# Attention operands laid out by DMA through DRAM instead of by selector matmuls, with the column visits in neighbouring slots

## What is computed

```python
def _L0_attn_b_ref(x, Wq, bq, Wk, bk, Wv, bv, Wo, bo):
    q = (x @ Wq + bq).reshape(Bx, Tx, HEADS, HD)     # HEADS 16, HD 8
    k = (x @ Wk + bk)[:, :, None, :]
    v = (x @ Wv + bv)[:, :, None, :]
    q = _apply_rope(q, sin, cos, HD)
    k = _apply_rope(k, sin, cos, HD)
    att = jnp.einsum('bthd,bThd->bhtT', q, k) / math.sqrt(HD)
    att = jnp.where(causal, -jnp.inf, att)
    att = jax.nn.softmax(att, axis=-1)
    out = jnp.einsum('bhtT,bThd->bthd', att, v).reshape(Bx, Tx, Cx)
    return out @ Wo + bo

def expert_step(acc, w):                             # 8 experts, 128 -> 512 -> 128
    wg, wu, wd = w
    h = jax.nn.silu(x @ wg) * (x @ wu)
    return (acc + h @ wd, None)

x = x + _L0_attn_a_ref(_layernorm(x, axis=-1), ...)
x = x + _L0_ffn_ref(_layernorm(x, axis=-1), ...)
x = x + _L0_attn_b_ref(_layernorm(x, axis=-1), ...)
x = x + _L0_ffn_ref(_layernorm(x, axis=-1), ...)
```

## Time and profile before

| | us |
|---|---|
| median of three runs | 1626.02 |
| time of the profiled execution | 1626.96 |
| its span from the first to the last instruction | 1625.1 |
| PE busy with matmuls | 1492.9 (92%) |
| DVE busy | 1174.6 (72%) |
| ACT busy | 885.4 (54%) |
| POOL busy | 793.0 (49%) |
| one steady pass of the second half (five alike) | 101.2 |

### The profile page before, as it was taken

How to read it: one execution, slowest core, us unless ns; L and a number is a source line. 1 busy time by engine, 2 the same in 40 slices (tenths; PEclk the granted TensorE clock), 3 DMA queues, 4 the chain that set the end, 5 groups by cost and what they waited for, 6 DMA issues and landing times. The chain is left out here.

```text
span 1625.1 us, 23329 instructions
## 1 busy us (share of the span) xinstructions
PE 1492.9 (92%) x7504; PEld 1108.8 (68%) x7504; DVE 1174.6 (72%) x1943; ACT 885.4 (54%) x1520; POOL 793.0 (49%) x738
## 2 busy tenths in 40 slices
PE   2578899899989999899999999999999999999998
PEld 2355677677776777677567676776767767677786
DVE  4768786968778787868677585675857758577565
ACT  2244646464555556444655557565575655755554
POOL 2636544642535344531315546555465554655565
PEclk9689999999999999999999999999999999999999
DMA  6305534333344343433332334333343333433452
GB/s 182 136 1 175 201 133 153 134 139 150 123 148 147 134 155 117 156 117 117 117 131 103 118 117 146 124 133 117 118 154 123 126 117 121 157 119 124 148 182 112
DMA packets 36236, 216.28 MB, mean 133 GB/s; under 512 B 3475, under 2 KB 17300, under 8 KB 19732
## 3 DMA queue, kind: packets, MB, share of 16 engines
q1 hardware_dynamic: 36116, 214.79, 36.4%
HBM read 200.10 MB, written 15.27 MB: 133 GB/s over the span
## 5 line engine op out<-in xcount | busy, mean ns | idle before, releaser
L530 POOL TENSOR_TENSOR HL<-HF,HH 128x512 fp32r<-128x512 f32 x312 | 416.8, 1336 | 474.3 <-ACT HH L706 473.2
L1213 DVE TENSOR_TENSOR HF<-SG,bank 128x512 f32<-128x512 f32 x512 | 350.0, 684 | 170.3 <-PE bank L874 90.4
L872 PE MATMUL bank<-XTH,W 128*128 128x512 f32 x1024 | 422.8, 413 | 10.4 <-ACT SG L699 9.9
L874 PE MATMUL bank<-XTH,W 128*128 128x512 f32 x1024 | 403.1, 394 | 0.0
L873 PE MATMUL bank<-XTL,W 128*128 128x512 f32 x1024 | 402.7, 393 | 0.0
L1196 DVE SCALAR_TENSOR_TENSOR SG<-SG,bank 128x512 f32<-128x512 f32 x288 | 197.1, 684 | 207.4 <-ACT SG L701 205.6
L701 ACT ACTIVATE SG<-bank 128x512 f32<-128x512 f32 x288 | 172.1, 597 | 317.8 <-PE bank L874 316.3
L706 ACT ACTIVATE HH<-HF 128x512 fp32r<-128x512 f32 x512 | 320.4, 626 | 36.4 <-DVE HF L1213 32.0
L699 ACT ACTIVATE SG<-bank 128x512 f32<-128x512 f32 x224 | 133.5, 596 | 250.7 <-PE bank L874 249.4
L872 PEld LDWEIGHTS bank<-XTH,W 128*128 128x128 f32 x1024 | 194.0, 189 | 82.0 <-issue 23.2
L872 PE MATMUL dbank<-HH,W 128*128 128x512 f32 x512 | 217.9, 426 | 16.1 <-DVE HL L1202 14.9
(11 more groups left out here) (212 smaller groups left out, 1796.4 us busy)
## 6 DMA issues: line engine op xcount, KB each, us to landing
W<-kept_w SPq DMA_DIRECT2D x120, 1536.0 KB, 6.3
kept_w<-W SPq DMA_DIRECT2D x8, 1536.0 KB, 6.2
X<-in_L_attn_a_x_dram SPq DMA_DIRECT2D x8, 256.0 KB, 5.4
WS<-in_L_ffn_Wg_dram SPq DMA_DIRECT2D x8, 256.0 KB, 6.5
WS<-in_L_ffn_Wu_dram SPq DMA_DIRECT2D x8, 256.0 KB, 6.8
WS<-in_L_ffn_Wd_dram SPq DMA_DIRECT2D x8, 256.0 KB, 7.3
out_dram<-X SPq DMA_DIRECT2D x8, 256.0 KB, 7.3
CST<-in_tables_dram SPq DMA_DIRECT2D x1, 898.0 KB, 5.4
```

Source lines behind the costliest of these rows:

```text
L530: g.tensor_tensor(HL[:, n % HRING, :], HF[:, n % HFRING, :], HH[:, n % HRING, :].bitcast(F32), ALU.subtract).then_inc(F.hl, 1)
L872: pe.matmul(dst, wh, xh, start=start, stop=False)
L874: return pe.matmul(dst, wl, xh, start=False, stop=stop)
L1213: v.tensor_tensor(HF[:, n % HFRING, :], gated, fbank[(2 * n + 1) % 3], ALU.mult).then_inc(F.mul, 1)
```

## The change

The selectors, both stacks and the operand `Q2` are gone. What they did is done by DMA through two small DRAM tensors.

- **Queries.** As soon as `QKH` is made, SP writes it to DRAM (256 KB). It then issues eight loads that put it into `QST` in the stacked layout, eight rows each (once as the first, once as the second copy). The low part `QKL` goes the same way with one store and four loads. In the plan SP does this at r = -8, -7 and -6.
- **Maxima.** DVE's `split_maxima` now writes the high and the low parts into a tile `NMS` with two instructions instead of four. PE transposes it once per sequence (`mx`, at r = 7 and r = 13, point 1). ACT copies 64 rows to `MT`, SP stores them with two DMAs, and one slot later four DMAs of two rows each load them into the free rows of `QST`. The column visits read `QST`, with 26 rows of each group; the row visits use 24 of the 32 rows.
- **Column visits** stand in neighbouring slots, all at point 2: r = 12 to 15 and 17 to 20 (before 12, 14, 15, 17 and 18, 20, 21, 23). ACT does the exponential of a visit first in the next slot, ahead of the gate's nonlinearity; before, it came behind it. `PT` is a ring of six visits.
- **Projections** come three slots sooner (`q` at r = -11), and the rotation, `QK` and `QKH` with them. `turn` is one slot later (r = -18). The values' products and the output come one to five slots sooner, `fturn` one slot sooner (r = 32).
- **Weights' loads** stand in SP's program one slot behind the down product that frees their place, in one order with the DMAs above. Their wait is the same.
- The buffers of attention B lie elsewhere in the arena, and two waits at its start are moved to fit.

```diff
-B_CELL = {"turn": (-19, 1, 3), "q": (-8, 2, 0), "qs": (-7, 1, 1), "k": (-7, 2, 2), "ks": (-6, 1, 0), "v": (-5, 1, 1),
...
-          ("stack", 0, 0): (7, 1, 3), ("stack", 0, 1): (9, 1, 3), ("stack", 1, 0): (14, 1, 3),
...
+B_CELL = {"turn": (-18, 1, 3), "q": (-11, 2, 0), "qs": (-10, 1, 1), "k": (-10, 2, 2), "ks": (-9, 1, 0),
+          "v": (-8, 1, 1), ("mx", 0): (7, 1, 3), ("mx", 1): (13, 1, 3), ("pv", 0, 0): (17, 1, 3),
...
-COLS_AT = [[(12, 2), (14, 0), (15, 2), (17, 0)], [(18, 2), (20, 0), (21, 2), (23, 0)]]
+COLS_AT = [[(12, 2), (13, 2), (14, 2), (15, 2)], [(17, 2), (18, 2), (19, 2), (20, 2)]]
+PT_RING = 6
...
+            def spread_queries(t, part, src, done):
+                for g in range(NG):
+                    to = RG * g + DB * part
+                    rows = kept_q[src, RG * g:RG * (g + 1), :].rearrange("(j x) t -> x j t", j=NJ)
+                    sp.dma_start(QST[to:to + DB, :, :].bitcast(F32), rows).then_inc(done, 16)
...
+            def side_b(t, r):
+                if r == -8:
+                    sp.wait_ge(B.hi, 2 * t + 1)
+                    after(sp, B.st_hi, 8 * 16 * t)
+                    sp.dma_start(kept_q[0], QKH[:, 0, :].bitcast(F32)).then_inc(B.hi_out, 16)
+                if r == -7:
+                    sp.wait_ge(B.hi_out, 16 * (t + 1))
+                    after(sp, B.t_ready, 8 * t)
+                    spread_queries(t, 0, 0, B.st_hi)
+                    spread_queries(t, 1, 0, B.st_hi)
+                    sp.wait_ge(B.lo, 2 * t + 1)
...
+                    sp.dma_start(kept_q[1], QKL[:, 0, :].bitcast(F32)).then_inc(B.lo_out, 16)
+                if r == -6:
+                    sp.wait_ge(B.lo_out, 16 * (t + 1))
+                    spread_queries(t, 2, 1, B.st_lo)
...
+            for slot in range(0, G_LAST + 1):
+                for t, r in b_tiles(slot):
+                    side_b(t, r)
+                for x in range(NE, 2 * NT * NE):
+                    u = FC * (x - WRING + 1) - 1
+                    if slot == ffn_slot(u // UNIT) + u % UNIT + LAG + 1:
+                        load_weights(x)
...
                 n = unit_of(slot)
-                if n is not None:
-                    gate_act(n)
...
                 for t, r in b_tiles(slot):
                     for b in range(SPT):
                         for i, (at, point) in enumerate(COLS_AT[b]):
-                            if r == at + (point == 2):
+                            if r == at + 1:
                                 exps(SPT * t + b, i)
+                if n is not None:
+                    gate_act(n)
...
+            def turn_maxima(n, b, bk):
+
+                pe.wait_ge(B.nml, n + 1)
+                pe.transpose(bk[0:64, 0:P], NMS[:, b, :].bitcast(F32), ident).then_inc(B.mx, 1)
```

More of the change, by code:

```diff
@@ L89 @@
 C_MASK = CPOS["mask_rows"][0]
-C_SEL = CPOS["qhi_0"][0]
-SELS = [f"q{p}_{j}" for j in range(NJ) for p in ("hi", "lo")] + ["eye"]
 UNIT = NE * FC
@@ L334, in program @@
         KST = take("KST", TOK, dt=F32R)
[L335 to L339, removed]
+        assert at["now"] <= r_at
+        PT = take("PT", 3 * PT_RING, TOK)
         OS = take("OS", 2, TOK)
@@ L496, in _, with load_weights @@
             sp.dma_start(BRAW[:, C:], row(b_bk)).then_inc(ld.wb, 16)
-            for x in range(NE, 2 * NT * NE):
+            def load_weights(x):
                 sp.wait_ge(F.down, FC * (x - WRING + 1))
@@ L776, in exps @@
             def exps(n, i):
+                m = (4 * n + i) % PT_RING
                 act.wait_ge(B.t_ready, 4 * n + i + 1)
-                after(act, B.pv, 2 * n)
-                act.activation(PT[:, 3 * i:3 * i + 3, :], three, ACT.Exp, scale=DB ** -0.5).then_inc(B.t_used, 1)
+                after(act, B.pv, 2 * (n - 1) if i < 2 else 2 * n)
+                act.activation(PT[:, 3 * m:3 * m + 3, :], three, ACT.Exp, scale=DB ** -0.5).then_inc(B.t_used, 1)
             def side_b(t, r):
@@ L811, in side_b @@
                             act.activation(OS[:, z, :], abank, ACT.Copy).then_inc(B.os, 1)
-                    for h in range(2):
-                        if r == B_CELL["stack", b, h][0]:
-                            act.wait_ge(B.q2_ready, 2 * n + h + 1)
-                            after(act, B.t_ready, 4 * (n - 1))
-                            act.activation(Q2[:, b, 2 * h:2 * h + 2, :], r3(sbank[bank_of(("b", t, ("stack", b, h)))], 2),
-                                           ACT.Copy).then_inc(B.q2_used, 1)
+                    if r == B_CELL["mx", b][0]:
+                        act.wait_ge(B.mx, n + 1)
+                        after(act, B.mt_out, 32 * (n - 1))
+                        act.activation(MT[0:64, b, :], sbank[bank_of(("b", t, ("mx", b)))][0:64, 0:P],
+                                       ACT.Copy).then_inc(B.mt, 1)
                     if r == B_CELL["ot", b][0]:
@@ L1083, in project_v @@
                 m.then_inc(B.v_ready, 1)
-            def query_stack(t, j, bk):
-                pe.wait_ge(B.lo, 2 * t + 1)
-                pe.matmul(bk, SELR[:, SQ + 2 * j, :], QKH[:, 0, :], start=True, stop=False)
-                pe.matmul(bk, SELR[:, SL + 2 * j, :], QKL[:, 0, :], start=False, stop=True).then_inc(B.st_ready, 1)
             def b_cell(t, name, dst):
@@ L1475, in _ @@
                 n = unit_of(slot)
+                if slot == b_slot(0):
+                    v.wait_ge(A.z, NT)
+                    v.wait_ge(A.done, NT)
                 new_maxima(slot, 2)
```

186 lines of the change are left out of this document (85 added, 101 removed), and 2 rows, old and new, of the table B_CELL.

## The result

The changed kernel takes 1645.62 us (median of four runs, 1643.89 to 1647.52), the kernel before beside it 1626.13. The ratio is 1.0125, with a 95% interval of 1.0113 to 1.0137. It is 1.25% slower, where 1597 was forecast.

The account below looks back on a forecast made before the run. PE, busy 92% of the span, was taken to bound the kernel. Work removed -35, waits gone -4.6, new waits +6.3 and weights +4 gave -29 us: 1597 us (chance 0.62), range 1581 to 1613.

Parts of the forecast that it names:

- the weights behind the layout on SP's queue: Weights' load of r = 27, needed at r = 32, arrives within half a microsecond of need; 0.5 us per tile, 4 us.
- rival C: Layout's issues on SP at 1.0 us each make the weights 6.1 us late; kernel slower, 1642 us; chance 0.08.
- nothing large is in the queue: Ground for short issues: the load of r = 23 lands 6.3 us after its issue, before the layout starts.
- The 18 us: By the skill's rule, twelve layout loads of about 2 us one behind the other make weights some 18 us late per tile.
- The rest of the sum: PE work taken off -35 us, waits that go at r = 13 and 14 -4.6, waits that come at r = 13 +6.3.
- The waits that come at r = 13: PE waits 0.6 us for the maxima's transpose and 0.3 before the second column visit; seven passes, 6.3 us.
- The other column visits: Each needs the exponential from one slot before; ACT's 2.3 us just fits PE's 2.5 us; counted as nothing.
- rival B: Exponential ahead of `SG` makes PE wait 0.45 us at each of eight visits, 29 us; time unchanged, 1626; chance 0.08.
- The maxima's DMAs: Stores and loads at r = 7 and r = 13 have five and four slots to land; neither is waited for.

Follow-up runs that it names:

- little data: Changed kernel, but from the second tile on every spread of the queries moves 64 of 512 columns (8 KB for 64 KB): 1602.93 us, ratio 0.9859.
- wide loads: Changed kernel, but from the second tile on each of the twelve spreads writes 32 neighbouring partitions with one row each: 1603.63 us, ratio 0.9869.

## Why the prediction was wrong

**The step that failed** is *the weights behind the layout on SP's queue*: 0.5 us a tile counted, 9.2 as its bound. From the start of r = 24 to the gate of r = 32 PE needs 20.1 us in the runs without this wait, close to the 19.9 forecast. In the pass shown above the load's way took 1153.36 - 1127.91 = 25.45, where 19.4 were forecast. Its terms:

| term | forecast | measured |
|---|---|---|
| to the end of `QKH`, and the first store's issue | 2.4 | 2.55 |
| high store | 2.5 | 2.04 |
| eight issues | 3.6 | 2.71 |
| wait for `QKL` | 0 | 0.67 |
| low store | 2.5 | 6.65 |
| four issues | 1.8 | 1.34 |
| weights' load | 6.3 | 9.49 |
| semaphores | 0.3 | not seen apart |
| sum | 19.4 | 25.45 |

The issues, on which the bound and rival C turned, were cheaper than forecast. The error is in two landings, 4.15 and 3.2 us. Both stand behind loads of the layout in the same DMA queue, and the prediction counted these loads' issues but no data at all. Two rows had misled it. That 64 KB land after 2.0 us was read from a load that writes 128 partitions, and was taken to hold for one that writes 8. And "nothing large is in the queue" was true of each load, but eight of them are 512 KB at 63 GB/s, 8 us. The two runs with little data and with wide loads show this directly: with as many issues the pass is 97.5 us.

**The range failed, and not its bound.** 9.2 us a tile, got from slow issues, would have held the 7.6 measured in that pass (105.1 - 97.5). But the range took in only 1.3 of them, on the ground that the issues are short. Of the 7.6 us, 5.4 are the wait (slot r = 31 lasted 7.63 us instead of 2.25). The other 2.2 come from the clock at 0.50 in r = 32, a price that the prediction had in no case.

**Rival C** was right on the place, on its sign and nearly on the time (1642), by another cause than its own: not 1.0 us an issue, but 0.34, and data that stood in the way. The rule of the Trainium skill (DMA: Bandwidth & Descriptors, section "Rules for kernel authors") that the prediction set against this layout was put aside because the overhead runs side by side. The overhead did so, eight issues in 2.71 us; the data did not. The 18 us that the prediction worked out from the rule were too much: the weights came 5.4 us late.

**The rest of the sum held.** Its best test is the kernel with four loads over 24 partitions, whose other engines' work is the changed kernel's.

- Without the weights' term the sum was -33 us. Measured are 1597.56 - 1626.16 = -28.6. A steady pass lost 3.7 us (101.2 to 97.5), where 4.4 + 0.77 - 0.9 = 4.3 were forecast. PE's busy time fell by 100.77 - 96.68 = 4.1, and its idle time rose from 0.4 to 0.8.
- The waits that come at r = 13 were put at 0.6 and 0.3. In the changed kernel they are 2.6 / 6 = 0.4 and 1.3 / 7 = 0.2, ended by DVE's subtraction and by `PT`, as said.
- The other column visits were counted at nothing, and rival B feared 0.45 each. No such wait came. The run with Exp behind shows that Exp ahead is what keeps the waits of the neighbouring slots small: 1.3 us over the run, against 16.0.
- The maxima's DMAs were counted at nothing. No wait of PE in the changed kernel names them.

That 1597 came out for another kernel is in part luck: 4 us too much gain in the sum stood against 4 us for the weights.

## What to carry to other kernels

A DMA that costs no engine time still has a price in its queue: add up the bytes that stand ahead of the next urgent load, at the rate of that shape of transfer, and not only the issues. Take the rate from a row that writes as many partitions and has the same first axis. A first axis of 2 or 4 held a transfer to as many engines; one of 16 brought all 16 to work, but over 16 partitions that was no faster than 13 engines over 24. Where a store or a load must land before an in-order engine may go on, put the urgent load ahead of the wait.

## What the hardware showed

- The rate of a load into SBUF went with the partitions that it writes, and not with the DMA engines at work. 2 KB rows into 8 partitions moved 63 GB/s with 8.5 engines, into 24 partitions 166 with 13, and into 16 partitions 111 with all 16, after a first microsecond at 234. The Trainium skill, SBUF — State Buffer, section "Door 1: The DMA port swizzle (why `[64,N]` ≈ `[32,N]`)", says that 16 ports share about 436 GB/s and that four neighbouring partitions lie on one port. By that, 8 partitions reach 2 ports, 16 reach 4 and 24 reach 6; an estimate from that page is 55, 109 and 164 GB/s. The runs agree, but for that first microsecond; none of them shows a port. Four partitions that lie 32 apart moved 59 GB/s, at the pace of their issues; what they can move is open.
- A transfer also runs on few DMA engines where its first axis is short: 2 entries kept 1.9 engines at work, 4 kept 4.2, 8 kept 8.5. Rows of 8 KB did not help against that.
- An issue on SP took 0.34 us for a load of 8 partitions, 0.45 for 32 partitions of one row each, 0.56 for 4 partitions 32 apart, and 0.7 for 24 partitions from three copies. Why was not tried.
- A store on ScalarE's queue sent nothing for 5.6 us while transfers from SP's queue, the load of 1.5 MB above all, filled the DMA engines.
- A wait of 5.2 us on PE cost 2.2 us more through the granted clock, which stood at 0.50 (1.2 GHz) over the first five microseconds of work behind it. Over six such waits of 4.4 to 5.4 us it was 1.3 to 2.6 us.
